# Four record and row buffers in place of two in the second edge pass of a graph network, and a loop body of eight iterations

## What is computed

```python
hid = jax.nn.silu(edge_scalars @ fc_w1 * _inv(R))
w = hid @ fc_w2 * _inv(FC_HID)
w1, w2, w3, w4, w5 = jnp.split(w, [64, 128, 160, 192], axis=-1)
es = h_s[edge_src]
ev = h_v[edge_src]
m_s1 = w1 * es * e0
m_s2 = w4 * jnp.einsum('eci,ei->ec', ev, e1) * _inv(3)
m_v1 = (w2 * es)[:, :, None] * e1[:, None, :]
m_v2 = w3[:, :, None] * ev * e0[:, :, None]
m_v3 = w5[:, :, None] * jnp.cross(ev, e1[:, None, :]) * _inv(2)
agg_s = jax.ops.segment_sum(mid_s, edge_dst, num_segments=n) * inv_nn
agg_v = jax.ops.segment_sum(mid_v, edge_dst, num_segments=n) * inv_nn
```

## Time and profile before

| | us |
|---|---|
| median of three runs | 18012.45 |
| lowest and highest run | 17975.47 and 18085.38 |
| the profiled execution | 17932.95 |
| its span, first to last instruction | 17931.1 |
| busy share of PE, DVE, ACT and POOL | 69%, 58%, 37%, 23% |
| mean granted clock of TensorE | 0.777 |

### The profile page before, as it was taken

One profiled execution on the slowest core, in us unless ns is written; L12 is line 12 of the kernel. 1 busy time (PEld: TensorE's weight loads), 2 busy tenths in 40 slices (PEclk: granted clock), 3 DMA queues, 4 the chain that ended last, 5 costly groups with the idle time before them and its releaser, 6 DMA issues. The chain is left out here.

```text
span 17931.1 us, 271904 instructions
## 1 busy us (share of the span) xinstructions
PE 12441.9 (69%) x57506; PEld 9273.9 (52%) x57507; DVE 10418.3 (58%) x31035; ACT 6615.3 (37%) x17353; POOL 4200.5 (23%) x4329
## 2 busy tenths in 40 slices
PE   2488888888888888888863555444457777777776
PEld 1355555555555555555543444433346666666666
DVE  3366666666666666666665555433346666666663
ACT  0244444444444444444430000000035555555552
POOL 0022221222222221222212222200024444444440
PEclk8688888888888888888875666655568888888888
DMA  1122221211111112212212333200023344343343
GB/s 25 33 43 42 43 42 41 43 42 43 41 42 42 42 42 43 43 41 43 42 49 77 77 76 76 56 16 16 16 67 121 122 124 126 122 124 122 123 123 104
DMA packets 1814491, 1146.35 MB, mean 64 GB/s; under 512 B 1159571, under 2 KB 1539385, under 8 KB 1814206
## 3 DMA queue, kind: packets, MB, share of 16 engines
q1 hardware_dynamic: 1640126, 817.73, 17.0%
q0 software_dynamic: 174336, 328.31, 7.7%
HBM read 677.41 MB, written 467.83 MB: 64 GB/s over the span
## 5 line engine op out<-in xcount | busy, mean ns | idle before, releaser
L613 POOL DMA_INDIRECT att_src<-src_table,att_idx x1768 | 1774.1, 1003 | 6811.1 <-DMA att_idx<-in_src_dst 5437.4
L1653 POOL DMA_INDIRECT conv_src<-conv_table,conv_pair x1864 | 1820.8, 977 | 2440.2 <-DVE conv_prod L1811 1742.3
L1739 ACT ACTIVATE conv_scaled<-conv_onehot,conv_pair 128x128 f32<-128x128 f32 x5592 | 1659.0, 387 | 1360.7 <-DVE conv_onehot L1777 1085.0
L663 PE MATMUL att_banks<-dst_feat,att_onehotT 128*128 x3528 | 982.6, 375 | 1308.0 <-issue 668.6
L1281 PE MATMUL attend_banks<-attend_wm,attend_onehot 128*128 128x168 f32 x3520 | 1010.7, 477 | 1099.1 <-DVE attend_onehot L1303 1099.1
L1281 PEld LDWEIGHTS attend_banks<-attend_wm,attend_onehot 128*128 128x128 f32 x3520 | 931.0, 321 | 1178.4 <-issue 1063.2
L663 PEld LDWEIGHTS att_banks<-dst_feat,att_onehotT 128*128 128x128 f32 x3528 | 589.4, 211 | 1747.9 <-issue 1747.7
L680 PE MATMUL att_banks<-att_w_last,att_hid 64*128 64x224 f32 x3528 | 1450.7, 499 | 12.8
L1682 PE MATMUL conv_banks<-conv_w_last,conv_hid 64*128 64x224 f32 x1858 | 671.1, 445 | 994.9 <-DVE conv_prod L1811 730.5
L694 PE MATMUL att_banks<-att_ident,att_ch 128*128 128x128 f32 (+1 forms) x5280 | 1242.6, 415 | 2.1 <-ACT att_chT L808 1.5
L965 DVE TENSOR_TENSOR att_m<-att_banks,att_src 128x320 f32<-128x320 f32 x882 | 430.3, 488 | 1318.2 <-PE att_banks L663 1318.1
(11 more groups left out here) (353 smaller groups left out, 28752.2 us busy)
## 6 DMA issues: line engine op xcount, KB each, us to landing
agg<-conv_acc SPq DMA_DIRECT2D x928, 288.0 KB
messages<-att_msg SPq DMA_DIRECT2D x440, 320.0 KB
attend_msg<-messages SPq DMA_DIRECT2D x220, 640.0 KB, 4.0
conv_pair<-in_conv_rec SPq DMA_DIRECT2D x936, 70.0 KB, 1.9
att_es<-in_esT SPq DMA_DIRECT2D x1776, 32.0 KB
conv_src<-conv_table,conv_pair POOLq DMA_INDIRECT x1864
att_idx<-in_src_dst SPq DMA_DIRECT2D x1768, 1.0 KB, 1.7
att_geo<-in_edge_vec SPq DMA_DIRECT2D x1768, 1.5 KB
```

Source lines behind the costliest of these rows:

```text
L613: g.indirect_dma_start(out=src[h][:, u, :], out_offset=None, in_=x_table[:, :], in_offset=bass.IndirectOffsetOnAxis(ap=idx[h][:, u, 0:1], ...
L663: last = t.matmul(banks[:, BM, n * FEAT:n * FEAT + FEAT], onehotT[:, u * P:u * P + P], dst_feat[:, bass.ds(b, 1), :].rearrange("p a f -> p ...
L1653: g.indirect_dma_start(out=src[h][:, u, 0, :], out_offset=None, in_=x_table[:, :], in_offset=bass.IndirectOffsetOnAxis(ap=ends[h][:, u // ...
L1739: last = s.activation(scaled[h][:, u, d, :], onehot[h][:, u, :], ACT.Copy, scale=geo[h][:, u // 2, u % 2, PLANE_AT[d]:PLANE_AT[d] + 1])
```

## The change

The buffers `pair` (records) and `src` (gathered rows) and their semaphores `rec_landed` and `src_landed` are rings of four in place of two. Records are loaded four iterations ahead in place of two. Rows are gathered two iterations ahead in place of one, after the same wait for `prod_done`. All other buffers (`hid`, `onehot`, `scaled`, `dot`, `keep4`) stay double. The loop of each engine has eight iterations in its body in place of two, and so 29 turns in place of 116; the number of iterations stays 232, and the step tables stay as long. Ahead of the loop SP loads records four times in place of twice, and POOL gathers twice in place of once.

```diff
+SLOTS = 4
+AHEAD = 2
+BODY = 2 * SLOTS
-        pair = [a.sb(f"pair{h}", [P, PAIR_ITER, P + 2 * REC]) for h in range(2)]
-        src = [a.sb(f"src{h}", [P, T, 2, CONV_ROW]) for h in range(2)]
+        pair = [a.sb(f"pair{q}", [P, PAIR_ITER, P + 2 * REC]) for q in range(SLOTS)]
+        src = [a.sb(f"src{q}", [P, T, 2, CONV_ROW]) for q in range(SLOTS)]
+        def turn_of(i, j):
+            return i * (BODY // SLOTS) + j // SLOTS
...
-                load(0, 0)
-                load(1, 1)
-                with sp.Fori(0, PAIR_ITERS // 2) as i:
-                    for h in range(2):
-                        it = 2 * i + h
+                for q in range(SLOTS):
+                    load(q, q)
+                with sp.Fori(0, PAIR_ITERS // BODY) as i:
+                    for j in range(BODY):
+                        it, q = BODY * i + j, j % SLOTS
                         hold(sp, sp_passed, (x_done, it + 1), (soh_done, it + 1), (src0_done, it + 1), (dot_done, it + 1),
-                             (src_landed[h], 16 * T * (i + 1)))
-                        load(it + 2, h)
+                             (src_landed[q], 16 * T * (turn_of(i, j) + 1)))
+                        load(it + SLOTS, q)
...
-                gather(0, 0)
-                with pool.Fori(0, PAIR_ITERS // 2) as i:
-                    for h in range(2):
-                        it = 2 * i + h
+                for q in range(AHEAD):
+                    gather(q, 0)
+                with pool.Fori(0, PAIR_ITERS // BODY) as i:
+                    for j in range(BODY):
+                        it = BODY * i + j
                         pool.wait_ge(prod_done, PAIR_ITER * it + 1)
-                        gather(1 - h, i + h)
+                        gather((j + AHEAD) % SLOTS, turn_of(i, j + AHEAD))
```

More of the change, by code:

```diff
@@ L1669, in _, with net_map @@
                 t = nc.tensor
-                def net_map(it, h, turn):
-                    pe.wait_ge(rec_landed[h], 16 * PAIR_ITER * (turn + 1))
+                def net_map(it, q, turn):
+                    pe.wait_ge(rec_landed[q], 16 * PAIR_ITER * (turn + 1))
                     if not isinstance(it, int):
                         pe.wait_ge(hid_done, it)
-                    t.matmul(banks[:, BX, :], net[:, :], es[h], start=True, stop=True).then_inc(x_done, 1)
+                    t.matmul(banks[:, BX, :], net[:, :], es[q], start=True, stop=True).then_inc(x_done, 1)
                 def edge_weights(g, h, n, it):
@@ L1711, in _ @@
                 edge_weights(0, 0, 0, 0)
[L1712 to L1715, removed]
+                with pe.Fori(0, PAIR_ITERS // BODY) as i:
+                    for j in range(BODY):
+                        it, h = BODY * i + j, j % 2
+                        net_map(it + 1, (j + 1) % SLOTS, turn_of(i, j + 1))
                         for n in range(PAIR_ITER):
@@ L1752, in _ @@
                 scale_sources(0, 0, 0)
-                with act.Fori(0, PAIR_ITERS // 2) as i:
-                    for h in range(2):
-                        it = 2 * i + h
+                with act.Fori(0, PAIR_ITERS // BODY) as i:
+                    for j in range(BODY):
+                        it, h, coming = BODY * i + j, j % 2, (j + 1) % SLOTS
                         hidden(it + 1, 1 - h)
-                        scale_onehots(it + 1, 1 - h)
-                        scale_sources(it + 1, 1 - h, i + h)
+                        scale_onehots(it + 1, coming)
+                        scale_sources(it + 1, coming, turn_of(i, j + 1))
             @block.vector
@@ L1762, in _, with one_hots @@
                 v = nc.vector
-                def one_hots(it, h, turn):
-                    dve.wait_ge(rec_landed[h], 16 * PAIR_ITER * (turn + 1))
+                def one_hots(it, q, turn):
+                    h = q % 2
+                    dve.wait_ge(rec_landed[q], 16 * PAIR_ITER * (turn + 1))
                     if not isinstance(it, int):
@@ L1840, in _ @@
                 products(0, 0, 0, 0)
-                with dve.Fori(0, PAIR_ITERS // 2) as i:
-                    for h in range(2):
-                        it = 2 * i + h
+                with dve.Fori(0, PAIR_ITERS // BODY) as i:
+                    for j in range(BODY):
+                        it, h, q = BODY * i + j, j % 2, j % SLOTS
+                        coming, turn = (j + 1) % SLOTS, turn_of(i, j + 1)
                         for n in range(PAIR_ITER):
```

69 lines of the change are left out of this document (36 added, 33 removed).

## The result

| | before | changed |
|---|---|---|
| median, lowest and highest run, us | 18025.61, 17975.47 and 18085.38 (4 runs) | 17843.92, 17797.70 and 17867.85 (4 runs) |
| profiled execution, us | 17932.95 | 17828.81 |

The ratio is 0.989, with a 95% interval of 0.9866 to 0.9913: the changed kernel took 182 us less, 1.0%.

The account below looks back on a forecast made before the run. It took a chain through several engines as the bound, 18.2 us an iteration. Leads counted 0, loop ends -26, fetches +55: 17933 gave 17962 us profiled, the median 18012 gave 18040 us. Range 17890 to 18240 us.

Parts of the forecast that it names:

- The floor of 14.99 us: One turn of the chain through PE, DVE and ACT, end to end of `scale_sources`, which no buffers shorten: 14.99 us.
- Nothing that the change brings earlier is late: Users of gathered rows and records on ACT, DVE and PE show 0.0 us idle; rows come some 6.8 us early.
- The two steps that I costed at 0: In the loop, gathering rows two iterations ahead and loading records four ahead: each a total of 0.
- The rival of a buffer late after all: Rows or records were late, so the rings bring the iteration to its floor: 17270 us, chance 0.03.
- POOL's wait for records goes: POOL's idle time put down to records, 102.7 us in 110 iterations, may go; nobody gains from it.
- The fetch term: Longer loop body fetched again each turn, one uncovered landing on DVE: 29 x 1.9 = 55 us, from 0 to 165.
- the rival of fetches on several engines: DVE pays three landings a turn and PE or ACT two, uncovered: 18262 us, chance 0.23.
- Fewer loop ends: 87 loop ends go on every engine, 0.30 us each: 26 us of gain, from 0 to 104.
- The 3.2 us of waits above the floor: Waits within PE, DVE and ACT that lengthen the mean iteration beyond the chain's turn, taken as untouched: 3.2 us an iteration.
- the gather bursts stop hurting: Longer lead loosens contention of gather, records and stores, half the waits go, 371 us: 17670 us, chance 0.11.
- The forecast's own range: Median of before less 104 us for loop ends to plus 165 us for fetches: 17908 to 18177 us.

Follow-up runs that it names:

- e7: The kernel before without the gathers of its loop (row buffers filled once ahead, sums over wrong rows): 17181.1 us, ratio 0.9661.
- e15: The changed kernel with a loop body of four, rings and both leads kept, second measurement: 17291.2 us, ratio 1.0139.
- e4: The changed kernel with both leads taken back (rows one, records two iterations ahead), rings of four and body of eight kept: 17796.2 us, ratio 1.001.
- e1: The changed kernel cut to its loop body of eight alone, with two buffers and the old leads: 17771.3 us, ratio 1.000.
- e3: The changed kernel with rows gathered one iteration ahead in place of two: 17786.1 us, ratio 1.0003.
- e18: The changed kernel with both leads taken back, rings of four and body of eight kept, third measurement: 17829.4 us, ratio 0.9934.
- e16: The changed kernel cut to its loop body of eight alone, two buffers and old leads, third measurement: 17854.3 us, ratio 0.9939.
- e17: The changed kernel with a loop body of four, rings and both leads kept, third measurement: 17841.9 us, ratio 0.9934.
- e13: The changed kernel cut to its loop body of eight alone, two buffers and old leads, second measurement: 17324.2 us, ratio 1.0123.
- e6: The kernel before, unchanged, run and profiled again against itself: 17779.8 us, ratio 0.9994.
- e9: The changed kernel with its gathers issued later, once the next iteration's one-hot matrices are there: 18729.9 us, ratio 1.0364.
- e10: The changed kernel with its gathers begun one products later, at a place in between: 18298.1 us, ratio 1.0122.
- e12: The kernel before with gathers of 64 bytes a row in place of 768, sums over wrong rows: 18090.5 us, ratio 0.9998.
- e8: The changed kernel with two buffers, the old leads and a loop body of four: 17818.4 us, ratio 1.0019.
- e14: The changed kernel with both leads taken back, rings of four and body of eight kept, second measurement: 17320.7 us, ratio 1.0036.

## Why the prediction was wrong, point by point

- **The floor of 14.99 us** was right. Without gathers an iteration takes 15.0 us (e7), and with them too where the bursts do no harm (15.09, e15). The changed kernel's shortest turn is 14.95 us.
- **Nothing that the change brings earlier is late** was right. The rows above show 0.0 us ahead of L1755, L1792, L1683 and L1781. The margin was read too large: the first user of the rows is `scale_sources` at 15040.26 and not `dots`, so they were there 2.1 us early in that iteration and not 6.8. And a record is loaded into a buffer that has just come free, as before, not into one free for two iterations. Neither slip changed the sum. Taking the leads away while keeping the rest gave the same on both occasions where they were run side by side with other variants: 1.001 beside 1.000 and 1.0003 (e4, e1, e3), 0.9934 beside 0.9939 and 0.9934 (e18, e16, e17). The two steps that I costed at 0 measured 0, within the 0.1 to 0.2% that these intervals leave. The rival of a buffer late after all (17270 us) fell with them.
- **POOL's wait for records goes** was right (102.7 us to none), and that nobody gains from it too.
- **The fetch term.** The mechanism was right: 12 packets a turn with a body of eight, none with four. The size, 55 us, could be seen only where the bursts are silent: 51 us between e13 and e15, of which 29 x 1.5 = 42 us are in the turns with the loop end. In the first profile of the changed kernel the iteration behind a loop end is 0.8 +- 0.3 us longer than the others, 23 us over 29 turns. In the medians it is not visible (1.000 with fetches beside 1.003 without, and 0.9939 beside 0.9934), so the term can be hidden there; the rival of fetches on several engines (18262 us, slower) fell. (Its deciding point, 206 us, is 3.7 landings a turn and not 3.6.)
- **Fewer loop ends, 26 us of gain:** too large for the loop end itself. Without gathers a turn with a loop end takes 15.02 us and one without 14.98 (e7), which is 3 us for 87 of them. The ground that ACT passes the loop end without a gap was read from the wrong row: L1746 stands in the middle of ACT's body, which begins with the silu, and that one did wait in before (0.7 us in e7):

```profile
L1731 ACT ACTIVATE conv_hid<-conv_banks 128x512 f32<-128x512 f32 x110 | 65.5, 595 | 243.1 <-remote 155.8 <-PE conv_banks L1675 58.1 <-issue 29.2
```

With gathers the loop end and the late hand-over meet, because DVE's loop end lies just ahead of the second `products`. In the first profile of before the turns with a loop end take 19.2 us and the others 17.4; measured from `dots` to `dots` the difference is 0.3 us, so the mark decides what is seen. In e6, where the change gained nothing, the two kinds of turn take 18.7 and 16.4 us.
- **The 3.2 us of waits above the floor, taken as a constant:** this is the step that failed. Its ground was *the gather, the load and the stores keep their triggers and so their places in the iteration*, and for it the rival *the gather bursts stop hurting* had 0.11. The ground itself held nearly: the trigger is the same, and the median gather begins 3.7 us ahead of the end of `scale_sources` in the first profile of before and 3.3 us ahead in that of the changed kernel. What didn't follow is that the waits stay. They are the bursts' (e7), as that rival said, and they came down from 3.3 to 2.8 us an iteration over the phase: 110 us, where the rival had assumed 371 and put its deciding point at 0.9 us an iteration. The link from the edge weights to the second `products` shrank from 3.91 to 3.16 us, and the one ahead of the first `products` grew from 0.41 to 0.61. So the truth was a part of the rival's effect, and some of it came without the rival's cause, the longer lead: a long body without any lead gained 0.6 to 0.7% (e16, e18). The forecast's own range left the middle out: it counted loop ends and fetches, not a seventh of the term that the waits are, 232 x 3.2 = 742 us.
- **The size of that term** I took from one profile. It is a matter of the occasion: 17.55 us an iteration of the same kernel in e6, and variants of it at 15.1 to 15.3 in e13 to e15. A range that rests on one profile can't hold that.

**Where the gain comes from.** Shown: the waits above the floor go with the gathers (e7). In the one pair of profiles that has both kernels on an occasion with a gain, 110 us less of these waits is the whole difference. A gain of 0.6 to 0.7% needs neither leads nor rings, and it is the same with the fetches and without (e16, e17, e18). It was there where before took 17952 us or more, and gone at 17786 and below. Shown too: the bursts' cost hangs on their place in the iteration (e9, e10) and not on their bytes (e12). Not settled: why a longer body lessens it. One reading is that a loop end adds to a hand-over that is late already. For it: the long turns of before are those with the loop end, and without gathers the loop end costs nothing. Against it: they stand out as much in e6, where the change gained nothing, and in e17, with a body of four, the turn with the loop end (17.9 us) is not the longest. The other reading is a shift between gather and chain. No run here tells them apart; the kernel before with a body of four (e8) on an occasion of 18000 us, profiled beside the kernel before, would be the next one to make. The variants gained 0.6 to 0.7% and the whole change 1.1 to 1.2%, but not on the same occasion, so whether the leads add something on a bad occasion is open as well.

No version that was run is better than both kernels on every occasion.

## What to carry to other kernels

Before a ring is deepened, read the idle time ahead of the first user of each buffer: at 0.0 us the deeper ring itself brings nothing, and that reading held on both occasions here on which leads and rings were taken away by themselves. But waits that no buffer explains are no constant either: price them by leaving the suspected work out (here 3.4% of the time went with the gathers), and count a part of that price into the range of any change that shifts the code around them. And a gain of 1% has to be measured on more than one occasion, with the kernel before beside it: this one was 1.2%, 0.7% in part, and nothing, by the occasion.

## What the runs showed of the hardware

- With gathers of eight indirect transfers in the loop, hand-overs between PE, ACT and DVE come late. In the kernel before, the second `products` begin 3.9 us on average after PE's edge weights, without gathers 0.9 us (e7). PE, ACT and DVE are all idle at once for 1.1 us in each iteration of before and 0.8 us in the changed kernel, most of it while POOL issues the second half of the gather, and 0.0 us without gathers. In e10 that is 0.0 us too, with 19.9 us an iteration, so it is not a measure of the whole cost. This is 2.6 to 3.3 us an iteration on most occasions and 0.1 us on one (e15). Rows of 64 bytes cost the same as rows of 768.
- The same kernel took from 17264 to 18096 us by the occasion (medians of 8 runs or more), with runs within 0.7% of each other on all but the fastest one; the same chip number gave 17786 and 17952 us.
- A loop body that is fetched again at each turn, 12 packets of 8 KB, cost 1.4 to 1.5 us in the turn with the loop end, and 1.8 us a turn of the loop in all, where it could be compared with a body that stays loaded (e13 and e14 against e15). A loop end without a fetch cost 0.04 us where no gather disturbed it (e7).
